# One gather per expert tile by a permutation inverted on TensorE, and a memory-to-memory copy at the end

## The reference

```python
h = layernorm(x) * (1 + ca) + sa
x = x + ga * attention(h)      # a recurrence over 256 steps, 16 heads of 8x8 states, then o @ Wo
h = layernorm(x) * (1 + cb) + sb
logits = h @ router_w + router_b
e = argmax(softmax(logits))    # one of 8 experts for each row
a, g = split(h @ w1[e])        # 128 -> 2 x 512
y = (silu(a) * g) @ w2[e]      # 512 -> 128
x = x + gb * max_prob * y
```

## Time and profile before

| | |
|---|---|
| Median of the timed runs | 517.53 us |
| Profiled execution, span from first to last instruction | 543.5 us |
| PE busy | 389.4 us (72%) |
| DVE busy | 414.1 us (76%) |
| ACT busy | 272.0 us (50%) |
| POOL busy | 276.2 us (51%) |
| Mean granted TensorE clock | 0.840 |

### The profile page before, as it was taken

How to read it: one execution, slowest core, us unless ns; L and a number is a source line. 1 busy time by engine, 2 the same in 40 slices (tenths; PEclk the granted TensorE clock), 3 DMA queues, 4 the chain that set the end, 5 groups by cost and what they waited for, 6 DMA issues and landing times. The chain is left out here.

```text
span 543.5 us, 8910 instructions
## 1 busy us (share of the span) xinstructions
PE 389.4 (72%) x2643; PEld 352.1 (65%) x2643; DVE 414.1 (76%) x1196; ACT 272.0 (50%) x600; POOL 276.2 (51%) x323
## 2 busy tenths in 40 slices
PE   2957555969677799450968664879999338999980
PEld 1322115969677699450968663879999238999980
DVE  5679999996999978999998996685957013548733
ACT  2688749663144244554555461453755026555620
POOL 1174329699999674537379375002223743232430
PEclk9988775868977787975889776789999759999996
DMA  8367859900000009203100012024130111233205
GB/s 206 60 70 122 117 105 144 113 1 1 0 2 1 0 8 378 82 0 50 29 2 0 1 35 60 20 39 99 41 107 25 55 54 40 77 91 94 60 29 159
DMA packets 50205, 35.01 MB, mean 64 GB/s; under 512 B 10992, under 2 KB 46608, under 8 KB 50032
## 3 DMA queue, kind: packets, MB, share of 16 engines
q1 hardware_dynamic: 47152, 29.07, 27.5%
q0 software_dynamic: 3008, 5.40, 3.2%
HBM read 15.26 MB, written 10.27 MB: 47 GB/s over the span
## 5 line engine op out<-in xcount | busy, mean ns | idle before, releaser
L570 PE MATMUL bank<-prod_o,ID 128*128 128x128 f32 x512 | 85.5, 336 | 41.3 <-POOL prod_o L287 18.0
L921 POOL DMA_INDIRECT placed_y<-Q,place x46 | 44.1, 958 | 126.0 <-ACT Q L1226 60.6
L570 PEld LDWEIGHTS bank<-prod_o,ID 128*128 128x128 f32 x512 | 79.9, 246 | 43.1 <-POOL prod_o L287 18.8
L718 PE MATMUL bank<-Q,p 128*128 128x128 f32 x736 | 96.5, 280 | 0.0
L718 PEld LDWEIGHTS bank<-Q,p 128*128 128x128 f32 x736 | 91.6, 196 | 0.1
L280 POOL TENSOR_TENSOR prod_o<-Q,ST 128x1024 f32<-128x1024 f32 x28 | 62.5, 2231 | 42.4 <-PE bank L574 29.1
L1063 ACT ACTIVATE p<-S,GAM 128x64 f32<-128x64 f32 x126 | 47.6, 410 | 70.6 <-DVE S L1498 68.0
L1219 ACT ACTIVATE p<-big 128x1024 f32 x46 | 48.5, 1057 | 54.8 <-PE bank L718 36.9
L1498 DVE TENSOR_REDUCE S<-p 128x64 f32<-128x320 f32 x126 | 55.4, 474 | 6.5 <-ACT p L1063 6.0
L1485 DVE TENSOR_REDUCE U<-p 128x32 f32<-128x288 f32 x128 | 52.7, 439 | 0.2 <-DVE p L1479 0.2
L1479 DVE TENSOR_TENSOR p<-S,bank 128x256 f32<-128x256 f32 x128 | 49.2, 407 | 0.7 <-ACT bank L1058 0.7
(11 more groups left out here) (225 smaller groups left out, 786.7 us busy)
## 6 DMA issues: line engine op xcount, KB each, us to landing
big<-in_L_ffn_w_dram SPq DMA_DIRECT2D x1, 4096.0 KB, 13.1
big<-big SPq DMA_DIRECT2D x16, 192.0 KB, 4.5
Q<-sorted_h SPq DMA_DIRECT2D x46, 64.5 KB, 2.0
sorted_h<-ZERO SPq DMA_DIRECT2D x2, 1472.0 KB, 16.4
X<-in_L_attn_x_dram SPq DMA_DIRECT2D x8, 256.0 KB, 4.8
big<-big SPq DMA_DIRECT2D x16, 128.0 KB, 4.9
X<-Q SPq DMA_DIRECT2D x32, 64.0 KB, 2.4
K<-placed_y SPq DMA_DIRECT2D x8, 256.0 KB, 3.0
```

The lines of the kernel that those rows point to most:

```text
L570: pe.matmul(ps, ID[:, :], prod_o[:, k % 2, i, :], start=(i == 0), stop=False, skip_group_check=True)
L718: m = pe.matmul(bank[(1, 6)[g % 2] + k][:, c * P:(c + 1) * P], W1E[g % 2][:, f:f + P], XST[:, g % 3, :], start=True, stop=True)
L921: pool.indirect_dma_start(placed_y[g // NF], bass.IndirectOffsetOnAxis(ap=place[:, g:g + 1], axis=0), YS[:, g % YR, :], None).then_inc(sem ...
```

## The change

Nothing is sorted through memory any more. The rows stay in their order in `rows_h`, 385 numbers wide: the normalized row, its probability, the row of x after the attention half, and its gb. For each expert tile an indirect DMA gathers 128 such rows. The list of rows comes from inverting the permutation: DVE builds two one-hot matrices from the places (`one_hots`: the tile number by a rounding trick, then 128x368 twice and 128x512 four times), PE multiplies them (`invert`, 16 matmuls of 128x23 into one bank), and DVE turns the sum into two index tables (`indices`). Row 2048 of `rows_h` is a spare row that padding points at. The result is finished inside the tile (`gate_y`, `add_x1`) and scattered to its own row of `placed_y`, or to one of the spare rows behind them. One memory-to-memory copy per slice, 16 pieces of 64 KB, brings `placed_y` into the output. SP no longer loads tiles; POOL issues 7 gathers ahead of the loop and then a scatter and a gather per tile. `ys` is gone from ACT.

```diff
+        def store_rows(queue, s, h):
+            queue.wait_ge(sem("h2_evac"), 4 * s + 2 * (h + 1))
+            queue.wait_ge(sem("maxp_set"), NHALF * s + h + 1)
+            queue.dma_start(rows_t[s][:, HB * h:HB * (h + 1), 0:D1], H2[s][h][:, :, :]).then_inc(sem("rows_in", s), 16)
+        def store_x1(queue, s):
+            queue.wait_ge(sem("x1_ready", s), 4)
+            queue.dma_start(rows_t[s][:, :, D1:D1 + D], XG[s]).then_inc(sem("rows_in", s), 16)
...
@@ SP
-            for g in range(NTIME * NF):
...
-                sp.dma_start(XS[:, g % XR, :], sorted_h[s][j * P:(j + 1) * P, :]).then_inc(sem(f"xs_in{g % XR}"), 16)
...
+            for s in range(NTIME):
+                if s == 1:
+                    for h in range(NHALF):
+                        move_outputs(sp, 1, [h])
+                store_x1(sp, s)
+                for h in range(NHALF):
+                    store_rows(sp, s, h)
+            for s in range(NTIME):
+                for r in range(YR):
+                    sp.wait_ge(sem(f"ys_out{r}"), 16 * len(range(r, (s + 1) * NF, YR)))
+                sp.dma_start(out_t[s], placed_y[s][0:SPARE, :].rearrange("(b p) d -> b (p d)", p=P)).then_inc(sem("stored"), 16)
@@ PE
+            def invert(s):
+                for t in range(NT):
+                    if t % 4 == 0:
+                        pe.wait_ge(sem("ohp_ready"), 4 * s + t // 4 + 1)
+                    m = pe.matmul(RANK_BANK[s][:, 0:NF], OHP[:, t, :], OHT[:, t, :], start=(t == 0), stop=(t == NT - 1))
+                m.then_inc(sem("inv_ps"), 1)
...
+                if g == PG:
+                    invert(0)
...
                 if g >= 1:
-                    pe.wait_ge(sem("ys_ready"), g)
+                    pe.wait_ge(sem("y_gated"), g)
...
+                if g == F_ROUTE + 2:
+                    invert(1)
@@ POOL
+            def gather(g):
+                s, j = divmod(g, NF)
+                if j == 0:
+                    pool.wait_ge(sem("idx_ready"), 2 * (s + 1))
+                    pool.wait_ge(sem("rows_in", s), 16 * (NHALF + 1))
+                    pool.wait_ge(sem("rows_fixed", s), 16 * 5)
...
+                if g >= XR:
+                    pool.wait_ge(sem("ys_ready"), g - XR + 1)
+                pool.indirect_dma_start(XS[g % XR], None, rows_h[s],
+                                        bass.IndirectOffsetOnAxis(ap=idx[s][:, 0, j:j + 1], axis=0)).then_inc(sem(f"xs_in{g % XR}"), 16)
...
+            for g in range(XR):
+                gather(g)
             for g in range(NTIME * NF):
...
+                scatter(g)
+                if g + XR < NTIME * NF:
+                    gather(g + XR)
@@ DVE
+            def one_hots(s):
+                yield from settle(dve.tensor_scalar(hi[:, :], posf[:, :], 1.0 / P, (1 - P) / (2.0 * P), ALU.mult, ALU.add))
+                yield from settle(dve.tensor_scalar(hi[:, :], hi[:, :], WHOLE, None, ALU.add))
+                yield from settle(dve.tensor_scalar(hi[:, :], hi[:, :], -WHOLE, None, ALU.add))
+                yield from settle(dve.scalar_tensor_tensor(out=lo[:, :], in0=hi[:, :], scalar=-float(P), in1=posf[:, :], op0=ALU.mult, op1=ALU.add))
...
+                for q in range(4):
+                    qt = [P, 4, P]
+                    dve.tensor_tensor(OHP[:, 4 * q:4 * q + 4, :], lo[:, 4 * q:4 * q + 4].unsqueeze(2).broadcast_to(qt),
+                                      UNIT[:, :].unsqueeze(1).broadcast_to(qt), ALU.is_equal).then_inc(sem("ohp_ready"), 1)
+                    yield
...
+            def gate_y(g):
                 dve.wait_ge(sem("y_ps"), g + 1)
                 if g >= YR:
                     dve.wait_ge(sem(f"ys_out{g % YR}"), 16 * (g // YR))
+                row = XS[g % XR]
+                dve.scalar_tensor_tensor(out=YS[:, g % YR, :], in0=bank[3][:, 0:D], scalar=row[:, D:D1], in1=row[:, D1 + D:RD],
+                                         op0=ALU.mult, op1=ALU.mult).then_inc(sem("y_gated"), 1)
+            def add_x1(g):
+                dve.wait_ge(sem("y_gated"), g + 1)
+                dve.tensor_tensor(YS[:, g % YR, :], YS[:, g % YR, :], XS[g % XR][:, D1:D1 + D], ALU.add).then_inc(sem("ys_ready"), 1)
...
@@ DVE, loop over g: gate_y(g - 3), xst(g + 2), add_x1(g - 3), ...
                 if g == F_ROUTE + 1:
                     now(sort(1))
                     now(sorted_places(1))
+                    now(one_hots(1))
+                if g == F_ROUTE + 2:
+                    now(probability(1))
+                    now(tiles_experts(1))
                 if g == F_ROUTE + 3:
-                    now(tiles_experts(1))
+                    indices(1)
...
                 if g < G:
                     gate_u(g)
```

More of the change, by code:

```diff
@@ L16 @@
 O_EPS = 1e-6
+WHOLE = 1.5 * 2.0 ** 23
 def adaln_block(nc, x, Wq, Wk, Wv, Wo, Wbet, Wf, norm_w, router_w, router_b, w1, w2, c, wmod, out):
@@ L457, in _ @@
             for s in range(NTIME):
-                rows = sorted_h[s].rearrange("(n p) d -> p n d", p=P)
-                sp.dma_start(rows[:, :, 0:D], ZERO[:, :].unsqueeze(1).broadcast_to([P, NF, D])).then_inc(sem("padded", s), 16)
-                with nc.allow_non_contiguous_dma(reason="places of the padding rows"):
-                    sp.dma_start(rows[:, :, D:D1], PLACES[:, :].unsqueeze(2)).then_inc(sem("padded", s), 16)
+                for start in range(0, RD, P):
+                    size = min(P, RD - start)
+                    sp.dma_start(rows_h[s][SPARE:SPARE + 1, start:start + size], ONES[0:1, 0:size]).then_inc(sem("rows_fixed", s), 16)
+            sp.wait_ge(sem("gates_out"), 16)
+            for s in range(NTIME):
+                sp.dma_start(rows_h[s][0:SPARE, D1 + D:RD].rearrange("(b t) d -> b t d", b=B),
+                             gate_h.rearrange("(b d) -> b d", b=B).unsqueeze(1).broadcast_to([B, P, D])).then_inc(sem("rows_fixed", s), 16)
             for h in range(NHALF):
@@ L1658, in first_slice_rows @@
                 yield from sorted_places(0)
+                yield from one_hots(0)
                 yield from tiles_experts(0)
+                yield from after_chunk(AT_SORT + 4)
+                yield from probability(0)
             def between():
@@ L1680, in _ @@
                 make_products(dve, NG - 1, h)
+            indices(0)
             G = NTIME * NF
```

181 lines of the change are left out of this document (54 added, 127 removed).

## The result

The changed kernel takes 544.13 us (median of four runs, 542.88 to 544.77) against 518.59 us for the kernel before (four runs, 517.5 to 520.34). The ratio is 1.0476, with a 95% interval of 1.0429 to 1.0524. It is slower by 25.5 us; I had forecast 16.6. Three of the four runs of the kernel before are those the forecast started from.

What follows compares the result with a forecast made beforehand. The prediction took DVE to bound the recurrence and PE the loop. Its terms, 4.2 + 0.2 + 3.0 + 12.0 + 0.3 + 2.0 - 5.1 = +16.6 us on 517.5, gave 534 us, range 521 to 545.

Steps and rivals of the forecast that it cites:

- the frame: Whole kernel: the timed runs lack the profile's delays, so the forecast starts from 517.8 us against a median of 517.5.
- The gap of 26.0 us: Profiled span 543.5 against median 517.5: put down to profile-only delays under two scatter bursts, summing to 25.7 us.
- Rival (a): The delays under the scatter bursts are in the timed runs too, so the change gives 508 us; chance 0.10.
- the first delay: Under the first scatter burst, DVE sat idle 3.93 us after PE finished group 13, before make_products(14, 1).
- Recurrence, +4.2: Slice 0's one_hots and probability fall on a fully busy DVE, adding 4.2 us; invert(0) on PE costs nothing.
- Hand-over, +0.2: From recurrence to loop: the first gather, behind indices(0), lands 2.9 us after POOL's start, adding 0.2 us.
- Rival (b): In the loop, gathers land late and set the period, deciding from 3.3 us on: 543 to 544 us; chance 0.15.
- Slice 0 of the loop, +3.0: PE's second waits for gate_y behind DVE's other work, 0.5 us in each of six iterations: 3.0 us.
- The inversion of slice 1, +12: At gate_u(14), DVE's one_hots stall PE 6.5 us; slow restart and invert(1)'s 32 records bring it to 12.0 us.
- Change of slices, ring and contention, +0.3 and +2.0: Slice change and drain add 0.3 us; tight gather slots 0.5 and slice 0's output copy 1.5, together 2.0.
- POOL being locked out by DVE: DVE's two-port mode could block POOL's descriptor writing; the trace was said to disagree, 16 issues keeping 0.95 to 0.96 us.
- Tail, -5.1: From last scatter to end, 13.6 us becomes 8.5, with 5.0 for the output copy: a saving of 5.1 us.

Runs made afterwards that it cites:

- the undisturbed profile: The kernel before, unchanged, profiled a second time: span 515.2 us, time 517.01 us.
- the first three edited kernels: The changed kernel with, one at a time, slice 1's inversion spread, the x store in eight pieces, ACT freeing the result bank: 539.85, 539.52, 539.13 us.
- The experiment: The changed kernel with slice 1's 1024 KB store of x cut into 8 DMAs, each issued at another result: 539.52 us, ratio 1.0409.
- the ACT copy: The changed kernel with ACT copying results 0 to 13 out of PE's bank and gate_y working on the copy: 539.13 us, ratio 1.0401.
- The spread version: The changed kernel with slice 1's one_hots spread over iterations 14 to 17 and invert(1) moved from 15 to 18: 539.85 us, ratio 1.0429.

## Why the prediction was right, and where its sizes were off

The sign and the frame were right, and so was what the largest term said of PE's wait; three sizes were not, and one term came out by luck. 544.13 lies 0.9 us below the upper end of the range of 521 to 545 and above the 529 to 539 that the forecast gave to its own terms, so the number was close to a miss, and nearly all misses go the same way. It was luck, too, that the comparison fell where before takes 517 to 520: on the three other chips the changed kernel takes 556.9 to 561.1 us. Point by point:

**The gap of 26.0 us.** I took out 25.7 us and forecast from 517.8. A run without the gaps has 517.01, so the step held, and it decided the sign: counted as a gain, it would have given 508. That 25.7 met 26.0 was partly luck: I took a span against a time; span against span it is 543.5 - 515.2 = 28.3. What I took for its cause was wrong. Rival (a), that the delays are in the timed runs, is false for the comparison of the result and true on three chips; and even there dropping the bursts doesn't bring its gain, since the changed kernel is slower by 2.3%: it saves before's 28 us (543.5 against 515.2) and has 11 to 15 us of its own. For the first delay I had 3.9 us, read from DVE's idle time; laid beside the undisturbed profile it is 7.4 (350.79 - 330.29 = 20.5 against 13.1).

**Recurrence, +4.2.** Measured +4.3. The mark lies 0.5 to 0.9 us later in the first three edited kernels, so this agreement is within the scatter of one execution. `invert(0)` was hidden, as said: PE was idle for 3.00 us behind it.

**Hand-over, +0.2.** Measured +0.4. The first gather landed 347.53 - 344.09 = 3.4 us after POOL's start; I had 2.9 from the line between two loads. The Trainium skill ("DMA: Bandwidth & Descriptors", "Anatomy of one DMA — SWDGE (gpsimd) path") prices it at 2.0 us plus bytes over 436 GB/s, an estimate of 2.45, and the trace does not agree: the shortest of the 46 gathers took 3.0. Their median is 3.3 (3.2 for the 26 that go into PD), the very 3.3 at which, by my own sum, the ring starts to set the period, and the period in slice 1 stayed near 2.8 (transposes at 484.48 and 487.33) but for waits of 0.2 to 0.6 us. Rival (b) gave 543 to 544, which is the time that came, but by another way: what is late there is single gathers behind stores of 1 MB, not all of them.

**Slice 0 of the loop, +3.0.** Measured +5.7. This is the first term that failed, and by an omission. I had counted the contention of the output copy and not that of `store_x1`, which the edit shows just as well: 1024 KB that go on the engines at 378.02, 0.4 us ahead of a gather whose tile PE wants 3.8 us later and which lands after 8.5. The experiment gives it 3.8 us. The remaining 1.9 against my 3.0 is no proof of the mechanism I gave: `second(k)` waiting for `gate_y(k - 1)` is worth 0.2 by the ACT copy, and PE doesn't wait longer than before, it works at a lower clock (busy 54.3 us for 52.0). The reason for that stays open.

**The inversion of slice 1, +12.** Measured +17.5, the other size that was off. The parts: PE's wait 6.17 for my 6.5; `second(13)` at half clock +1.0 for 0.9; `invert(1)` 6.86 us for the 4.0 to 4.6 that I took; and then two of `hidden` and one `second` at half clock, 1.0 + 0.9 + 0.8 = 2.7. Sum 16.7, and one gather late by 0.63. So the wait was right in place and size, and what I mis-sized is how much of PE's work falls at the low clock behind it: I had 0.9 lost in one `second` and 0.6 more, and it was everything from 425.56 to 439.55. The upper end of my own term said "14 if half clock covers the inversion whole". It did, and it went on past it. I had put the low clock down to the standstill alone; by the runs above it goes with the narrow records as well, and which of the two keeps it down isn't shown. The spread version shows the price of the same 32 records at the full clock, 3.65 us.

**Change of slices, ring and contention, +0.3 and +2.0.** Measured +2.3 from `second(21)` to the last scatter. That the sum fits is luck for the larger part. To the transpose of tile 27 it is 9.0 us in both, so the change of slices cost nothing, and the +2.3 lie behind it. The 1.5 us were meant for the output copy of slice 0, but that goes out at 466.10 and lands after 5.6 us, while PE works without a gap until 475. PE's waits for gathers in this stretch, 1.3 us in all, come later; the rest isn't assigned. The prediction also says that the trace speaks against POOL being locked out by DVE: nine or ten of the 16 issues lie beside a busy DVE and keep their length, but no run shows in which mode DVE worked there, so it was no test of that.

**Tail, -5.1.** Measured -3.5. Issue of the copy 2.6 us after the last scatter (for 2.2 + 0.4), the copy 5.3 (for 5.0), and then 2.2 us in which SP waited for PE's queue before the end, for my 0.3. That is the third size; the 0.6 of the drain fall ahead of the last scatter and don't belong here (1.9 + 0.3 - 0.6 = 1.6). The waits of SP in the tail:

```profile
SPq L85 <- DMA out_dram<-placed_y: 4.6, 1, 4.6
SPq L85 <- PEq L85: 2.2, 1, 2.2
```

In the second profile of before the same two rows have 1.9 and 0.2.

The sum of the misses: 2.7 in slice 0, 5.5 in the inversion, 1.6 in the tail, 0.3 in the rest, together 10.1; 16.6 + 10.1 = 26.7, against 26.8 between the two profiles.

## What to carry to other kernels

When a step writes its rows to memory instead of keeping them on the chip, price its plain stores as rivals of the small transfers that the loop waits for: 1 MB in one DMA made PE wait 4.7 us for one gather, and in eight pieces, each let go by another iteration, 0.5. A block of DVE operations that makes PE stand still costs its length, and what PE does at the lower clock behind it has to be read from the trace and not guessed from the standstill: here 6.2 us of wait and some 7 us lost to the low clock, elsewhere 12.1 us of wait and under 2 us lost. Spread the block, or let another engine free the buffer that PE needs. And before a gap between profile and median is used, profile the kernel a second time: the frame was right here, the reason for it was not.

## What the runs showed of the hardware that was not expected

- The kernel before takes 517 us on one chip and 545 to 546 on three, with a spread of under 1% on each; each was used once. On the latter a waiter starts up to 2 us after PE's last record in the changed kernel (467.29 against 465.46), where in the first profile after it starts at once (460.75 against 460.71). In the first profile of before, which looks like these, it is 19.8 us for DVE under the second burst, and 7.4 us are lost under the first (the earlier trace rows against its second profile), while POOL issues indirect DMAs one behind the other.
- Once PE had stood for 6.2 us, its granted clock was at the lower level (0.50 of 2.4 GHz) for 14 us of uninterrupted work, the inversion's 32 records among it: 6.86 us against 3.65. Once it had stood for 12.1 us it was so for 3.4 us of work without such records. And it fell to 0.50 at the end of the inversion in a run where PE hadn't stood still for more than 1.3 us.
- 32 records of 128x23 take 3.65 us at the full clock. Eight of 128x128 take 1.06 and sixteen 1.95, which makes 3.73 for 32 (an estimate on the line between the two), so a narrow output saves next to nothing.
- A gather of 128 rows of 1540 bytes takes 3.3 us from issue to landing in the median and 3.0 at the least, a scatter of 512-byte rows 2.3. Issued 0.4 us behind a store of 1024 KB, a gather took 8.5.
- In the recurrence DVE stayed busy all the time (12.00 of 12.00 us) with the new operations in it, and PE, busy 9.74 us for 7.51, had 52 records for 46 at a granted clock of 0.55 for 0.78 (the earlier trace rows has the line before):

```profile
316.00:328.00 12.00, 9.74 (x52) 9.63 (x51) 12.00 (x36) 6.02 (x25) 0.00 (x0) 0.55 0.22 58
```
